# A relational graph layer on one core: products from a ring of five tiles in place of a staging copy, and another plan for the rows that SP fetches

## The reference, cut to what matters

```python
# x: (12500, 256) fp32; src, dst, edge_type: (212500,) int32, edges sorted by dst
h = jnp.maximum(_layernorm(x, axis=-1), 0.0)
hx = jnp.einsum('ni,rio->rno', h, weight)            # weight: (8, 256, 256)
agg = jax.ops.segment_sum(hx[edge_type, src], dst, num_segments=12500)
out = x + agg * 0.5 ** 0.5 + h_bias + (h @ loop_weight) * 0.5 ** 0.5
```

## Time and profile before

| | |
|---|---|
| median of 3 executions | 2087.11 us |
| the profiled execution | 2085.94 us |
| its span, first to last instruction | 2084.1 us |
| POOL busy | 1546.1 us (74%) |
| PE busy, matmuls | 1542.8 us (74%) |
| DVE busy | 1321.9 us (63%) |
| ACT busy | 529.2 us (25%) |
| mean granted clock of PE | 0.875 |

### The profile page before, as it was taken

The page is one execution under the profiler, slowest core; times in us unless marked ns, Lnnn a source line. Parts: engine busy times, 40 slices in busy tenths (PEclk is TensorE's granted clock), DMA queues, the critical chain, the costliest instruction groups (busy, mean ns, idle before and its releaser), DMA issues.

```text
span 2084.1 us, 40498 instructions
## 1 busy us (share of the span) xinstructions
PE 1542.8 (74%) x10568; PEld 1190.6 (57%) x10568; DVE 1321.9 (63%) x4144; ACT 529.2 (25%) x525; POOL 1546.1 (74%) x1631
## 2 busy tenths in 40 slices
PE   0027788788888778788788788787788787778777
PEld 0015566666666666566566566565566565666556
DVE  7755666666666666666766666766756665756552
ACT  5731321321321321321312312312312222312120
POOL 7777777777777777777777777777777777777772
PEclk9999888888898898888988888889888898888898
DMA  9964444444444444444444444444444444444441
GB/s 357 336 220 121 130 124 131 131 124 131 131 124 131 131 122 132 130 124 131 132 123 131 131 124 131 131 124 131 131 124 131 125 130 130 123 129 131 118 131 53
DMA packets 137080, 290.37 MB, mean 139 GB/s; under 512 B 36190, under 2 KB 80986, under 8 KB 133774
## 3 DMA queue, kind: packets, MB, share of 16 engines
q0 software_dynamic: 77904, 212.83, 35.2%
q10 hardware_dynamic: 44034, 51.22, 7.2%
q1 hardware_dynamic: 14908, 23.71, 3.5%
HBM read 262.02 MB, written 25.60 MB: 138 GB/s over the span
## 4 chain that ended last, share of the span: by engine, by line
POOL 34%; PE 21%; issue 15%; SPq 15%; DMA 13%; DVE 1%; ACT 1%; DVEq 0%; POOLq 0%; ACTq 0%
POOL rows L391 33%; PE psum L892 13%; SPq L317 12%; DMA rows<-h_table,src_i 8%; PE psum L957 5%; DMA h_table<-room 4%; SPq L312 3%; PE psum L897 1%; PE psum L885 1%; DMA rows<-h_table 1%; DMA room<-x 1%; PE psum L943 1%; ACT psum L457 1%; DVE room L758 0%; DVE stats L582 0%
## 5 line engine op out<-in xcount | busy, mean ns | idle before, releaser
L391 POOL DMA_INDIRECT rows<-h_table,src_i x1527 | 1451.4, 950 | 472.7 <-issue 431.1
L758 DVE TENSOR_TENSOR room<-room,psum 128x256 f32 x1661 | 696.4, 419 | 635.8 <-PE psum L957 552.0
L892 PE MATMUL psum<-w_sb,room 128*128 128x256 f32 x3072 | 1028.2, 454 | 11.0 <-DVE result L722 11.0
L957 PE MATMUL psum<-onehot,rows 128*128 128x128 f16 x6260 | 666.6, 237 | 407.6 <-DMA rows<-h_table,src_i 344.3
L957 PEld LDWEIGHTS psum<-onehot,rows 128*128 128x128 f16 x6260 | 478.5, 106 | 698.6 <-DMA rows<-h_table,src_i 458.1
L892 PEld LDWEIGHTS psum<-w_sb,room 128*128 128x128 f32 x3072 | 607.4, 225 | 64.5 <-ACT room L484 8.6
L484 ACT COPY room<-room 128x2048 f32<-128x2048 f32 x96 | 182.3, 1898 | 1328.4 <-DVE room L758 1277.0
L697 DVE TENSOR_SCALAR onehot<-lane,base_i 128x128 f16<-128x128 f16 x1565 | 428.4, 275 | 64.4 <-DVE room L758 0.5
L486 ACT COPY room<-zeros 128x2048 f32<-128x2048 f32 x96 | 182.3, 1899 | 3.1
L897 PE MATMUL psum<-w_sb,own_hT 128*128 128x256 f32 x384 | 121.4, 399 | 0.0
L380 POOL DMA_INDIRECT raw<-x,src_i x96 | 93.7, 976 | 31.3 <-issue 29.0
(11 more groups left out here) (55 smaller groups left out, 304.0 us busy)
## 6 DMA issues: line engine op xcount, KB each, us to landing
rows<-h_table SPq DMA_DIRECT2D x4864, 1.0 KB
rows<-h_table,src_i POOLq DMA_INDIRECT x1527
own<-h_table ACTq DMA_DIRECT2D x97, 128.0 KB
own_x<-x ACTq DMA_DIRECT2D x97, 128.0 KB
out<-result ACTq DMA_DIRECT2D x97, 128.0 KB
room<-x SPq DMA_DIRECT2D x12, 1024.0 KB, 7.2
h_table<-room ACTq DMA_DIRECT2D x12, 1024.0 KB, 7.3
w_sb<-weight SPq DMA_DIRECT2D x2, 1024.0 KB
```

The costliest lines, as they stand in the source:

```text
L391: nc.gpsimd.indirect_dma_start(out=rows[:, q % NB, :], out_offset=None, in_=table[:, :], in_offset=bass.IndirectOffsetOnAxis(ap=src_i[:, c ...
L758: nc.vector.tensor_tensor(window, window, sum_of(c).rearrange("p (a w) -> p a w", w=W), ALU.add).then_inc(added, 1)
L892: nc.tensor.matmul(ps_out[:, 0:D], stage[:, m, :], w_sb[:, h, r, :], start=(m == 0), stop=False)
L957: last = nc.tensor.matmul(sum_of(c)[:, h * P:(h + 1) * P], now[:, part * D + h * P:part * D + (h + 1) * P], onehot[:, k, :], start=(part = ...
```

## The change

The staging copy and its semaphore wait are taken out, and PE reads the tile in the ring. The ring has five slots instead of four, in the same SBUF room. The clear of a tile waits for its product and is issued behind the store of the tile. The offset of a window, node mod 512 before, is node mod 640, by a multiplication and a shift. The plan for SP has three chunks in eight steps, 36 in all (steps 3, 11, ... 91; 6, 14, ... 94; 8, 16, ... 96), so that POOL has 1529 gathers.

```diff
-    RING = 4
+    RING = 5
+    TILE_BITS = 7
+    FIFTH, FIFTH_BITS = 205, 10
...
-    SYNC_STEPS = [range(4, STEPS - 1, 5), range(6, STEPS - 1, 5)]
+    SYNC_STEPS = [range(3, STEPS - 1, 8), range(6, STEPS - 1, 8), range(8, STEPS - 1, 8)]
...
-        room = sb("room", [P, HR * (SPAN + W) + HR * P], fp32)
+        room = sb("room", [P, HR * (SPAN + W)], fp32)
...
-            def stage_tile(t):
-                act.wait_ge(added, chunks_before(t + 2))
-                if t % RING == 0:
-                    act.wait_ge(merged, spills_before(t + 1))
-                if t > 0:
-                    act.wait_ge(out_ready, t)
-                nc.scalar.copy(stage[:, :, :], ring[:, :, ring_slot(t):ring_slot(t) + P]).then_inc(staged, 1)
-                act.wait_ge(staged, t + 1)
+            def clear_tile(t):
+                act.wait_ge(out_ready, t + 1)
                 nc.scalar.copy(ring[:, :, ring_slot(t):ring_slot(t) + P],
                                zeros[:, :].unsqueeze(1).broadcast_to([P, HR, P])).then_inc(cleared, 1)
...
                 for t in range(TILES - 2):
-                    stage_tile(t)
+                    if t >= 1:
+                        store_tile(t - 1)
+                        if t <= TILES - RING + 1:
+                            clear_tile(t - 1)
                     copy_hT(t)
                     own_tile(t + 2)
-                    if t >= 1:
-                        store_tile(t - 1)
                     own_x_tile(t + 1)
...
-                nc.vector.tensor_scalar(offsets[:, :], step_base[:, :], SPAN - 1, None, ALU.bitwise_and
+                nc.vector.tensor_scalar(offsets[:, :], step_base[:, :], TILE_BITS, None, ALU.arith_shift_right
                                         ).then_inc(s_offsets, 1)
+                dve.wait_ge(s_offsets, 1)
+                nc.vector.tensor_scalar(offsets[:, :], offsets[:, :], float(FIFTH), None, ALU.mult
+                                        ).then_inc(s_offsets, 1)
+                dve.wait_ge(s_offsets, 2)
+                nc.vector.tensor_scalar(offsets[:, :], offsets[:, :], FIFTH_BITS, None, ALU.arith_shift_right
+                                        ).then_inc(s_offsets, 1)
+                dve.wait_ge(s_offsets, 3)
+                nc.vector.scalar_tensor_tensor(offsets[:, :], offsets[:, :], -float(SPAN), step_base[:, :],
+                                               ALU.mult, ALU.add).then_inc(s_offsets, 1)
...
-                    if k == 0 and s > 2:
-                        dve.wait_ge(cleared, s - 2)
+                    if k == 0 and s >= RING - 1:
+                        dve.wait_ge(cleared, s - RING + 2)
...
             def tile_product(t, m):
                 if m == 0:
-                    pe.wait_ge(staged, t + 1)
+                    if t % RING == 0:
+                        pe.wait_ge(merged, spills_before(t + 1))
                     if t > 0:
                         pe.wait_ge(scaled, t)
-                product(t, m)
+                product(t, m, ring[:, :, ring_slot(t):ring_slot(t) + P])
```

More of the change, by code:

```diff
@@ L130, in relational_graph_layer @@
         ring = room[:, 0:HR * (SPAN + W)].rearrange("p (m n) -> p m n", m=HR)
-        stage = room[:, HR * (SPAN + W):].rearrange("p (m n) -> p m n", m=HR)
+        stage = room[:, 0:HR * P].rearrange("p (m n) -> p m n", m=HR)
         rows_room = rows[:, :, :].rearrange("p k d -> p (k d)").bitcast(fp32)
@@ L151, in relational_graph_layer @@
         target = raw[:, G + 5, 0:1].bitcast(i32)
-        zeros_row = room[:, HR * (SPAN + W):]
+        zeros_row = room[:, 0:HR * P]
         NSUM = 6
@@ L689, in _ @@
             judge()
-            dve.wait_ge(s_offsets, 1)
+            dve.wait_ge(s_offsets, 4)
             def make_onehot(c):
@@ L748, in vector_step @@
                             engines=[mybir.EngineType.DVE], min_val=0, max_val=SPAN - 1,
-                            skip_runtime_bounds_check_because="offset = node % (RING * P), whatever the node")
+                            skip_runtime_bounds_check_because="offset = node % (RING * P) for a node below N")
                     if c == 0:
@@ L887, in last_products, with product @@
                 last.then_inc(out_ready, 1)
-            def product(t, m):
+            def product(t, m, nodes):
                 if m < HR:
                     h, r = m // R, m % R
-                    nc.tensor.matmul(ps_out[:, 0:D], stage[:, m, :], w_sb[:, h, r, :], start=(m == 0), stop=False)
+                    nc.tensor.matmul(ps_out[:, 0:D], nodes[:, m, :], w_sb[:, h, r, :], start=(m == 0), stop=False)
                 else:
@@ L996, in general_tile @@
                 for m in range(HR + H):
-                    product(t, m)
+                    product(t, m, stage)
             pe.wait_ge(s_unfit, 5)
```

## The result

The changed kernel takes 2073.28 us, the median of 4 executions (2071.29 to 2073.75), where the kernel before now has 2086.96 us (2085.65 to 2088.41, 4 executions). The ratio is 0.9932 (95% interval 0.9915 to 0.995): 14 us or 0.7% faster. The forecast was 2076.7 us, 10.4 us faster; the direction and the places were right, the size was 3 to 4 us too small.

What follows compares the result with a forecast made beforehand. POOL's gathers were taken to pace the loop, with SP a second bound whose last chunk left PE's backlog at the end. An earlier tail made the span 10.4 us less, 2073.7 us; taken off the median, 2076.7 us, range 2073 to 2083.

Steps and rivals of the forecast that it cites:

- SP's plan: SP's row fetches: SP gains 6.5 us in eight steps, third chunk tightest at 17 us early, PE's 8 waits go.
- POOL's stalls: Gather row on POOL: 6.6 us of stalls go, two more gathers cost 2.5 us, net 4.1 us earlier.
- The tail: Step 97 to the end: products start at 2041.6 us, step ends at 2053.9 us, then 19.8 us more.
- the clock: PE's products in step 97: 2.5 us lost at the lower clock, bounds 0 and 4.9 us.
- An unbroken row would start the last one: POOL's gathers at 1.2557 us each: last starts at 2043.2 us unbroken before, 2045.7 us after the change.
- I apply the difference to the median: Last step of the sum: 10.4 us taken off the median 2087.11 us, 1.2 us above the profiled execution.
- The staging copy: ScalarE's 96 copies, 182.3 us, removed: booked at nothing, as PE's waits for gathers cover any gain.
- The clear: Clear on ScalarE moved behind the store in step t+3: its wait already met, cover 16 chunks or 18 us.
- DVE's part: VectorE: merges from 25 to 20, 3.5 us hidden under idle time; extra offset and list operations before 127 us.
- One: Rival: only the two extra gathers show, the 6.6 us being POOL's own: 2089.6 us; chance 7%.
- Two: Rival: the new plan does not free SP, fetches reach 53.0 us and SP stays last: about 2087 us; 5%.
- Three: Rival: PE's weight loads slow down in a tile others write, at twice a load's mean: 2375 us; chance 8%.

Runs made afterwards that it cites:

- e1: The kernel before, unchanged, run once more for the spread of the gathers' pace: 2086.93 us, one execution.
- e12: The changed kernel with 32 chunks for SP instead of 36, 1533 gathers: 2077.51 us, 0.9962 of the kernel before.
- e4: The changed kernel, unchanged, run again on the chip of the first series: 2072.51 us, 0.9934 of the kernel before.
- e2: The kernel before with only SP's new plan of 36 chunks, staging copy and ring of four kept: 2072.51 us, 0.9937 of the kernel before.
- e5: The changed kernel with 32 chunks for SP, on a chip where the kernel before takes 3036.89 us: 2732.93 us, 0.8997 of it.
- e8: The changed kernel with a 37th SP chunk and earlier last-step products, where the kernel before takes 3036.89 us: 3002.6 us, 0.9902 of it.
- e7: The changed kernel with step 97's products from its third chunk, where the kernel before takes 3036.89 us: 2942.1 us, 0.9718 of it.
- e3: The kernel before with the ring of five and products straight from it, SP's old plan of 38 chunks kept: 2084.28 us, 0.999 of the kernel before.

## Why the prediction was right in its places and too small in its size

**SP's plan: right.** No wait for SP's rows is left, and the first chunks were in time. The third fetch was the tightest, as worked out, and nothing came of it. One detail was wrong: SP was to run into its buffers' limit and show gaps. It doesn't, at 50.2 us a fetch over 36 of them: eleven periods behind the tightest fetch the lead has only grown to about 17 + 11 x 6.5 = 89 us, at SP's last fetch. The gaps came with 32 chunks.

**POOL's stalls: right.** Their excess is gone (6.6 us by the first trace; by e1, at its quicker pace, 2049.89 - 2040.4 = 9.5 us), and two gathers more cost what a gather costs, as e12 shows at the other end.

**The tail: right, term by term.** Six gathers behind the sixth chunk, about 3 us for a gather to be used, 2.5 us for the clock, 19.8 us for the rest. In the changed trace the gather of the sixth chunk started at 2043.83 - 6 x 1.2532 = 2036.3 us and its chunk was taken at 2039.55 us, 3.2 us on; from there to the matmuls of L882 it is 12.75 us, where 0.4 + 9.75 + 2.5 = 12.65 us plus the 0.2 us between loads and matmuls had been booked. Two readings of the clock were less sound than this. The upper bound of its loss, 4.9 us, is too low: work that takes 9.75 us at 2.4 GHz takes 19.5 us at 1.2 GHz and loses 9.75 us. And the kernel before pays too, in some executions: in e1 the same stretch took 11.64 us, 1.7 us more than in its first trace. That 2.5 us fitted so well is in part luck. The rule of the Trainium skill ("TensorE: Matmul & The Clock Gate", section "HAM oscillation — how this bites in real kernels") agrees with this: the burst behind the waits started at the low clock, with 2.87 us for six matmuls where later ones take 1.51 us. The waits in front of it were short, 0.49 to 1.31 us each, shorter than those of the example on that page.

**The step that failed** is "An unbroken row would start the last one, 1526 later, at 127.03 + 1916.2 = 2043.2 us", and with it the new row's end at 2045.7 us. The term is the pace of a gather, 1.2557 us, taken from one execution, the slowest of ten. The changed kernel's trace has 1.2532 us, 3.8 us less over 1528 gathers. The terms against that trace:

| term | forecast us | measured us | difference us |
|---|---|---|---|
| start of the first gather | 127.03 | 128.96 | +1.9 |
| 1528 gathers | 1918.7 | 1914.9 | -3.8 |
| last gather to the loads of L882 | 8.2 | 8.3 | +0.1 |
| from there to the end | 19.8 | 19.9 | +0.1 |
| span | 2073.7 | 2072.0 | -1.7 |

The median was missed by 3.4 us, twice as much. The rest is the last step of the sum, "I apply the difference to the median": 1.2 us were added because the median of three executions lay that far above the profiled one. In the changed kernel the median lies 0.5 us below the profiled execution, and the kernel before itself has medians of 2085.75 us (15 executions) and 2085.69 us (9) on two chips, no higher than the 2085.94 us of its profiled execution. These 1.6 us (1.17 and 0.47) are, as far as the runs show, the spread of single executions and no effect of the change.

The end of the kernel before was set by SP and the backlog behind it, not by the pace of the gathers: e1, at 1.2527 us a gather, ends at 2085.2 us of span, and the first trace, at 1.2557 us, at 2084.1 us. The end of the changed kernel does depend on the pace. So the slow pace of that one execution went into the new time in full and was in no term of the old time against which the difference was taken. The same sum from e1: last gather 128.83 + 1528 x 1.2527 = 2042.9 us, the sixth chunk's gather 2035.4, products at 2038.8 (measured in e4: 2038.99), end of the step 2051.1, span 2070.9 us. e4 has 2071.2 us. The form of the sum was right and its base was not. The difference of the spans, e4 against e1, is 14.0 us, of which 1.7 us is e1's lower clock in step 97; that of the medians on that chip is 13.2 us.

The range did hold the pace, "as much above 1.2557 moves the end by 3.4 us either way", yet its lower end of 2073 us took the pace's bound alone and nothing for the 1.2 us that had been added for the median. The 1.2535 us of that bound stands in no row; the later traces came out on both sides of it.

**The staging copy: right.** It was booked at nothing, and e2 keeps it at the same time. **The clear: right**; DVE shows no wait for it in the changed kernel. **DVE's part: right**: the 20 merges, the offsets and the lists left no trace in the time: e4 and e2, which has the old merges and offsets, have the same median. ScalarE's longer zeroing took 5.3 us where 5.4 had been worked out.

**The rivals.** One fell by the result and by e2: the end moved when SP's plan alone was changed. Two fell on the chips where the kernel before takes about 2086 us, but happened on the chip of e5 to e8, where a fetch of 74.5 us is well over its threshold. Three fell with 190 ns as the median of the loads (columns: minimum, median, maximum; see the earlier trace rows):

```profile
L898 PEld LDWEIGHTS psum<-w_sb,room x3072: 190/190/338, 178.3 to 2050.7; 128*128 128x128 f32 x192
```

## What to carry to other kernels

Where a change moves the bound from one resource to another, work the new end out from the new resource's pace over several executions: the old time does not contain that pace, so an execution that is slow in it looks no slower. Take the old time, too, from more than one execution before a few microseconds are added for the median. Between two resources that each work without a rest, a plan that gives the tighter one 5% less (36 fetches for 38) was worth more here than the work it moved to the other, because the tighter one's lateness came out at the end as a backlog. And a copy on an engine that waits for its input 1277 us of 2084, and for which others wait only 8.6 us, went without a gain.

## What the runs showed of the hardware

A fetch of 128 rows by SP took 50.2 us on two chips and 74.5 us on a third (e7, whole fetches), with the gathers' busy time there at 949 ns, for 947 to 950; the kernel before took 3037 us there for 2086. On that chip a MOVE in SP's queue took up to 1419 ns, for 38 at most elsewhere, at the same median of 29 ns. The pace of POOL's indirect DMAs, the same instruction more than 1500 times, differed by 0.24% between two executions of the same kernel (1.2557 and 1.2527 us), and the first gather of an execution began between 126.64 us (e2) and 129.42 us (e3).
